# A three-norm macaron block in one software pipeline: the second FFN's gelu block and its products moved to other slots

## The chip, the cores and the metric

One core of a Trainium2 chip runs the whole program. The metric is the device time of one execution in microseconds (us), as the median over runs. TensorE (PE) multiplies matrices and writes to PSUM, VectorE (DVE), ScalarE (ACT) and GpSimd (POOL) do the elementwise work, SyncE (SP) issues the DMAs. Each engine works through its own queue strictly in order and meets the others at semaphores. All arithmetic on these queues is float32, except the bias and one-hot products.

## The reference, cut to what matters

The input is 32 sequences of 256 tokens with 128 features. It passes a mixture-of-experts FFN, a Mamba block (a selective scan) and the same FFN again:

```python
x = x + 0.5 * ffn(layernorm(x))     # f1
x = x + mamba(layernorm(x))         # p: the selective scan
x = x + 0.5 * ffn(layernorm(x))     # f2, same weights as f1
# ffn: e = argmax(x @ Wg + bg)      (8 experts)
#      y = gelu(x @ W1[e] + b1[e]) @ W2[e] + b2[e]
# mamba: x_path, z = split(rmsnorm(x) @ in_proj); x_path = silu(conv4(x_path))
#      dt_x, B, C = split(x_path @ x_proj); dt = softplus(dt_x @ dt_proj + b)
#      h = exp(dt*A)*h + dt*x_path*B ; y = C.h + D*x_path      (16 states, 256 channels)
#      out = (y * silu(z)) @ out_proj + x
```

## The kernel before

The 8192 tokens are cut into 16 chunks of 512. A hand-written software pipeline of 23 iterations (`i0` from -4 to 18) works on several chunks at a time: in iteration i the scan of chunk i, the Mamba preparation of chunks i+1 and i+2, the first FFN of chunks i+2 and i+3, and the second FFN of chunks i-1 to i-3. A stage that belongs to chunk i+off carries that `off`, and it is left out where the chunk does not exist. So iterations 3 to 12 carry all stages, and the later ones carry fewer and fewer.

Each iteration has 16 slots. In slot s, VectorE scans two units (2s and 2s+1) of the 32 that a chunk has; each unit is 128 partitions by 512 tokens. A unit is one `tensor_tensor_scan` (line 759, or line 757 in the slots of `POOL_C` = 1, 3, 5, 9, 14) and one product with C (line 763 on VectorE; in the slots of `POOL_C` line 944 on GpSimd). The decay of a unit, exp(dt*A), is made by ScalarE (line 632) in one of three PSUM buffers `dA`, so ScalarE can be at most three units ahead of VectorE. In its own slot s, ScalarE makes the decays of slot s+1. GpSimd makes the input of the units two slots ahead (line 936). TensorE sums the states (`sum_states`, line 489): at its slot s it sums what VectorE did in slots s-3 and s-2.

Everything else is placed between the units by tables. `PE_AT` (from `STAGES`), `ACT_AT`, `DVE_AT`, `POOL_AT` and `SP_AT` say at which slot each engine's queue holds a stage; a value of s+0.5 is behind the units of slot s. Each entry of `STAGES` is (name, offset, PSUM bank, slot, place in the slot); the two banks `G` are reused in the order of that list, and a stage waits until its bank was read. Place 0 is ahead of the slot's `sum_states`, place 1 too, place 2 at the end of the slot.

The FFN computes all eight experts for all tokens, and a one-hot mask that is added through the bias makes seven of them vanish. For each expert e of FFN w (0 for f1, 1 for f2) TensorE makes a first product (lines 461 and 462) into the only PSUM buffer `PH`, and ScalarE copies it out to `hs` (a "take", line 597) before the next first product may start. When all eight are taken, ScalarE runs a gelu block (`gelus`): table load, gelu of experts 0 to 3, one take between them, gelu of experts 4 to 7, table load back to exp. Then TensorE makes eight second products (line 477, 8 matmuls each, and line 475 for the bias at e = 0), which VectorE adds to X (line 815). `W1_AT` holds for each expert (slot and place of the first product on TensorE, slot and place of the take on ScalarE, offset), `W2_AT` (slot, place, offset) of the second product.

Other stages named below: `z0`, `z1` are the products for silu(z); `silu` is ScalarE's block of two table loads and three silus (lines 655 to 658); `out` is the output product of the Mamba block (line 511), which waits for bank 0 to be read by the first silu, and which VectorE adds to X at 4.5; `bc` and `dt1`, `dt0` are the products for B, C and dt (line 451); `soft` is the softplus; `ln_*` are the transposes of a normalized chunk and `gate_*` the expert logits (line 531), which VectorE turns into the one-hot mask `oh_*`; `x1`, `x0` are the products in front of the convolution, whose `taps` are made by ScalarE (line 647) and VectorE (line 776).

Of the kernel before, what the change touches and what calls it, by code (L numbers as in the profile page):

```python
# [46 lines left out]

STAGES = [("ln_f1", 3, 0, 1, 0), ("gate_f1", 3, 1, 2, 1), ("z0", 1, 0, 2, 2), ("z1", 1, 1, 3, 2),
# [3 lines left out]
PE_AT = {name: at for name, _, _, *at in STAGES}  # L52
G_SEQ = [(name, bank, off) for name, off, bank, _, _ in sorted(STAGES, key=lambda stage: stage[3:])]
G_AT = {name: (bank, off) for name, bank, off in G_SEQ}

ACT_AT = {"ln_f1": 1.5, "silu": 4.0, "bc": 6.0, "dt1": 6.5, "dt0": 7.0, "soft": 7.0, "gelu_f2": 7.5,
          "ln_f2": 9.5, "ln_p": 13.5, "taps": 14.5, "gelu_f1": 15.5}
DVE_AT = {"gated1": 1.5, "y_f2": 1.5, "gate_f1": 3.0, "out": 4.5, "oh_f1": 6.0, "stats_f2": 5.0, "gated0": 9.5,
          "y_f1": 10.0, "stats_p": 10.5, "gate_f2": 11.0, "stats_f1": 12.0, "oh_f2": 13.0, "tap01": 15.0, "tap2": 15.5}
POOL_AT = {"root_f2": 6.5, "norm_f2": 7.0, "dt": 8.0, "dtx": 8.5, "root_p": 11.0, "norm_p": 12.0, "root_f1": 12.5,  # L60
           "norm_f1": 13.0}
SP_AT = {"x_out": 3, "x_in": 4, "bc": 6, "b0": 8, "dt": 9, "b1": 10, "c0": 10, "b2": 12, "c1": 12, "b3": 14, "dtx1": 14,
         "c2": 14, "dt1": 15, "c3": 15}
# [967 lines left out]
```

## Time and profile before

| what | value |
|---|---|
| median of 3 runs | 1492.56 us (1492.42 to 1492.58) |
| the profiled execution | 1495.2 us, of which 1493.4 us is the span |
| TensorE / VectorE / GpSimd / ScalarE busy | 83% / 71% / 71% / 59% of the span |
| mean granted TensorE clock | 0.849 of full speed |
| one iteration, output product to output product | 82.4 to 82.8 us (iterations 2 to 12) |

The span runs from the first to the last instruction; the 1.8 us around it belong to the execution's time. The profiled execution is 2.6 us above the median of the three runs. A busy share is over the whole span, with the filling and the draining of the pipeline in it.

### The profile page before, as it was taken

Reading aid. Unit: us, or ns where it says so; the run is one execution under the profiler, and the core shown is the slowest. Engines: PE = TensorE matmul, PEld = TensorE weight load, DVE = VectorE, ACT = ScalarE, POOL = GpSimd, SP = SyncE. Lnnn points to the kernel's source line nnn. Section 1 sums busy time; section 2 is a strip of 40 time slices with the busy share of each in tenths; the row PEclk is TensorE's granted clock in tenths of the full one; section 3 lists DMA queues with packets and bytes.
Section 4 is the critical chain, followed back from the end, with each engine's and each line's share of the span. In section 5 each row is a group of like instructions: output and inputs, shape, how many; then the busy total and the mean of one; then the engine's idle time right before and its main releaser. Section 6 shows DMA issues by size and latency. Waiting matters only on the chain.

```text
span 1493.4 us, 16302 instructions
## 1 busy us (share of the span) xinstructions
PE 1232.2 (83%) x5188; PEld 612.7 (41%) x5188; DVE 1061.7 (71%) x1713; ACT 874.2 (59%) x1171; POOL 1067.6 (71%) x900
## 2 busy tenths in 40 slices
PE   2777768889898989989898988899898978667677
PEld 1333314234443534445353444444353434333344
DVE  2022887887878787877878787878878776979910
ACT  0244656476666767575667667575756675474532
POOL 1026796978878788868788787878687886997600
PEclk9989876788888998888888889888888987978786
DMA  3005050413233231503232332305032322232000
GB/s 84 1 0 205 10 198 9 158 43 120 92 108 106 89 111 33 181 23 127 80 120 92 108 106 73 127 24 185 28 115 85 122 85 105 101 114 92 1 7 14
DMA packets 60405, 130.02 MB, mean 87 GB/s; under 512 B 7744, under 2 KB 26864, under 8 KB 52128
## 3 DMA queue, kind: packets, MB, share of 16 engines
q1 hardware_dynamic: 60320, 128.98, 25.1%
q8 instruction: 42, 0.69, 0.2%
q14 instruction: 43, 0.35, 0.1%
HBM read 106.94 MB, written 22.02 MB: 86 GB/s over the span
## 4 chain that ended last, share of the span: by engine, by line
PE 41%; ACT 24%; DVE 23%; issue 8%; POOL 3%; SPq 1%; ACTq 0%; DVEq 0%; DMA 0%; POOLq 0%
PE PH L462 12%; PE PY L477 9%; DVE dA L759 9%; PE G L451 9%; ACT hs L610 6%; ACT dA L632 5%; DVE hb L757 4%; ACT hs L597 4%; DVE hb L763 3%; PE PH L461 3%; ACT L614 3%; ACT L610 2%; PE Y L489 2%; PE G L511 2%; PE G L531 2%
## 5 line engine op out<-in xcount | busy, mean ns | idle before, releaser
L936 POOL TENSOR_TENSOR hb<-dtx_rep,bs 128x1024 f32<-128x1024 f32 x256 | 598.8, 2361 | 0.0
L759 DVE TENSOR_TENSOR_SCAN dA<-dA,hb 128x512 f32<-128x512 f32 x352 | 429.8, 1221 | 68.5 <-ACT dA L632 61.6
L632 ACT ACTIVATE dA<-dt_rep,A 128x512 f32<-128x512 f32 x512 | 342.2, 689 | 143.4 <-DVE hb L763 128.7
L597 ACT COPY hs<-PH 128x512 f32<-128x512 f32 x256 | 149.4, 584 | 388.2 <-PE PH L462 387.9
L462 PE MATMUL PH<-xnT,W 128*128 128x512 f32 x512 | 339.0, 749 | 0.0
L477 PEld LDWEIGHTS PY<-W,hs 128*128 128x128 f32 x2048 | 281.8, 208 | 101.2 <-issue 88.8
L477 PE MATMUL PY<-W,hs 128*128 128x128 f32 x2048 | 323.2, 304 | 0.0
L944 POOL TENSOR_TENSOR hb<-hb,cs 128x1024 f32<-128x1024 f32 x80 | 188.4, 2355 | 140.7 <-DVE hb L757 140.7
L763 DVE TENSOR_TENSOR hb<-dA,cs 128x512 f32<-128x512 f32 x352 | 243.5, 692 | 25.2 <-DVE dA L759 0.9
L757 DVE TENSOR_TENSOR_SCAN hb<-dA,hb 128x512 f32<-128x512 f32 x160 | 186.3, 1206 | 102.6 <-ACT dA L632 99.5
L489 PE MATMUL Y<-hb,Sel 128*32 128x512 f32 x1024 | 164.5, 716 | 19.8 <-POOL hb L944 10.4
L461 PE MATMUL PH<-ohT,Lm 24*128 24x512 bf16 x256 | 109.1, 426 | 83.4 <-ACT hs L597 82.7
L610 ACT ACTIVATE hs<-hs 128x2048 f32<-128x2048 f32 x64 | 121.3, 1909 | 0.4
L462 PEld LDWEIGHTS PH<-xnT,W 128*128 128x128 f32 x512 | 86.6, 212 | 68.3 <-issue 68.3
L461 PEld LDWEIGHTS PH<-ohT,Lm 24*128 24x128 bf16 x256 | 23.5, 92 | 219.7 <-ACT hs L597 147.0
L776 DVE SCALAR_TENSOR_TENSOR xs<-G,Wc,xs 128x506 f32<-128x506 f32 (+2 forms) x96 | 67.2, 742 | 65.0 <-ACT xs L647 62.7
L531 PE MATMUL G<-Wg,xnT 128*128 128x8 f32 x256 | 56.2, 348 | 64.2 <-ACT xnT L590 64.2
L881 POOL TENSOR_SCALAR neg<-mv 128x4 f32<-128x4 f32 x48 | 9.7, 203 | 127.3 <-DVE mv L744 127.3
L963 POOL TENSOR_TENSOR dt<-dt,sp 128x1024 f32<-128x1024 f32 x16 | 37.6, 2353 | 83.5 <-ACT sp L676 83.5
L531 PEld LDWEIGHTS G<-Wg,xnT 128*128 128x128 f32 x256 | 53.8, 309 | 94.3 <-ACT xnT L590 94.0
L489 PEld LDWEIGHTS Y<-hb,Sel 128*32 128x32 f32 x1024 | 22.7, 116 | 114.1 <-issue 86.6
L815 DVE SCALAR_TENSOR_TENSOR X<-PY,X 128x512 f32<-128x512 f32 x32 | 21.8, 682 | 60.8 <-PE PY L477 60.8
(85 smaller groups left out, 1190.7 us busy)
## 6 DMA issues: line engine op xcount, KB each, us to landing
dtx_rep<-dtx_rows SPq DMA_DIRECT2D x32, 1024.0 KB, 6.5
dt_rep<-dt_rows SPq DMA_DIRECT2D x32, 1024.0 KB, 8.2
bs<-bc_rows SPq DMA_DIRECT2D x64, 256.0 KB, 3.7
cs<-bc_rows SPq DMA_DIRECT2D x64, 256.0 KB, 4.5
dtx_rows<-dtx SPq DMA_DIRECT2D x32, 256.0 KB, 2.5
dt_rows<-dt SPq DMA_DIRECT2D x32, 256.0 KB, 2.6
X<-in_x SPq DMA_DIRECT2D x16, 256.0 KB, 3.0
out<-X SPq DMA_DIRECT2D x16, 256.0 KB, 2.4
```

The costliest lines, as they stand in the source:

```text
L461: nc.tensor.matmul(PH[:, :], Lm[:, e, :], ohT[:, w, :], start=True, stop=False)
L462: nc.tensor.matmul(PH[:, :], W1[:, e, :], xnT[:, w, :], start=False, stop=True).then_inc(ph_full, 1)
L477: last = nc.tensor.matmul(PY[:, P * j:P * (j + 1)], hs[:, w, e, P * j:P * (j + 1)], W2[:, e, :], start=False, stop=e == E - 1 and j == J - 1)
L489: last = nc.tensor.matmul(Y[D32 * g:D32 * (g + 1), :], Sel[:, :], hb[:, (2 * k + g // 2) % HR, g % 2], start=q == 0, stop=q == NQ - 1)
L597: nc.scalar.copy(hs[:, w, e, :], PH[:, :]).then_inc(ph_free, 1)
L610: nc.scalar.activation(a, a, ACT.Gelu).then_inc(gelu[w], 1)
L632: nc.scalar.activation(dA[u % NA][:, :], dt_rep[:, h, g, :], ACT.Exp, scale=A[:, h, g, q:q + 1]).then_inc(decay, 1)
L757: nc.vector.tensor_tensor_scan(x_in_hb, a, x_in_hb, 0.0, ALU.mult, ALU.add).then_inc(scan, 1)
L759: nc.vector.tensor_tensor_scan(a, a, x_in_hb, 0.0, ALU.mult, ALU.add).then_inc(scan, 1)
L763: nc.vector.tensor_tensor(x_in_hb, a, cs[:, q, :], ALU.mult).then_inc(prod, 1)
L936: nc.gpsimd.tensor_tensor(hb[:, s % HR], dtx_rep[:, h, 2 * m:2 * m + 2, :], bs[:, q, None, :].broadcast_to([P, 2, CH]), ALU.mult).then_inc ...
L944: nc.gpsimd.tensor_tensor(hb[:, s % HR], hb[:, s % HR], cs[:, q, None, :].broadcast_to([P, 2, CH]), ALU.mult).then_inc(prod_p, 1)
```

## The change

Only tables change. No instruction is added or removed. On ScalarE the gelu block of f2 moves from slot 7.5 to slot 10.5, and `bc` and `dt0` move half a slot ahead. On TensorE the eight second products of f2 move from slots 10 to 15 to slots 12, 13, 14, 15 and to slots 0 and 1 of the next iteration (offset -3); `bc`, `dt1` and `dt0` stand directly behind `out`; `z1` stands ahead of the slot's `sum_states`; the first product of expert 6 of f2 stands ahead of `out`, and a first product of f1 stands at the end of slot 10, with its take inside the moved gelu block. On VectorE the addition of f2 moves from 1.5 to 2.5, and SyncE's store of x follows it.

```diff
-STAGES = [... ("z1", 1, 1, 3, 2),
-          ("out", -1, 0, 4, 1), ("oh_f1", 3, 1, 5, 1), ("bc", 1, 0, 6, 0), ("dt1", 1, 1, 6, 1),
-          ("dt0", 1, 0, 7, 0), ...
+STAGES = [... ("z1", 1, 1, 3, 1),
+          ("out", -1, 0, 4, 1), ("oh_f1", 3, 1, 5, 1), ("bc", 1, 0, 5, 0), ("dt1", 1, 1, 6, 0),
+          ("dt0", 1, 0, 6, 1), ...
-ACT_AT = {"ln_f1": 1.5, "silu": 4.0, "bc": 6.0, "dt1": 6.5, "dt0": 7.0, "soft": 7.0, "gelu_f2": 7.5,
+ACT_AT = {"ln_f1": 1.5, "silu": 4.0, "bc": 5.5, "dt1": 6.5, "dt0": 6.5, "soft": 7.0, "gelu_f2": 10.5,
-DVE_AT = {"gated1": 1.5, "y_f2": 1.5, ...
+DVE_AT = {"gated1": 1.5, "y_f2": 2.5, ...
-SP_AT = {"x_out": 3, ...
+SP_AT = {"x_out": 4, ...
-W1_AT = [[(8, 2, 7, 3, 3), (9, 2, 9, 0, 3), *[(s, 0, s, 0, 3) for s in (10, 11, 12, 13, 14, 15)]],
-         [(15, 1, 15, 0, -1), (15, 2, 15, 1, -1), (15, 3, 15, 3, -1), (1, 0, 0, 0, -2), (2, 0, 2, 0, -2),
-          (3, 0, 3, 0, -2), (5, 0, 4, 2, -2), (6, 0, 6, 0, -2)]]
-W2_AT = [[(s, 1, 2) for s in (4, 6, 8, 8, 8, 9, 9, 9)],
-         [(s, k, -2) for s, k in ((10, 1), (11, 1), (12, 1), (13, 1), (14, 1), (14, 1), (15, 1), (15, 2))]]
+W1_AT = [[(8, 2, 8, 0, 3), (9, 2, 9, 0, 3), (10, 0, 10, 0, 3), (10, 2, 10, 3, 3),
+          *[(s, 0, s, 0, 3) for s in (11, 12, 13, 14)]],
+         [(15, 0, 15, 0, -1), (15, 1, 15, 1, -1), (15, 2, 15, 3, -1), (1, 0, 0, 0, -2), (2, 0, 2, 0, -2),
+          (3, 0, 3, 0, -2), (4, 0, 4, 0, -2), (5, 0, 6, 0, -2)]]
+W2_AT = [[(s, 1, 2) for s in (5, 7, 7, 8, 8, 8, 9, 9)],
+         [(12, 1, -2), (13, 1, -2), (14, 1, -2), (15, 2, -2), (0, 1, -3), (0, 1, -3), (1, 1, -3), (1, 1, -3)]]
```

## Rows read from the trace of the kernel before

**Rows 1.** The page's first part: busy time, share of the span, instructions.

```profile
span 1493.4 us, 16302 instructions
...
PE 1232.2 (83%) x5188; PEld 612.7 (41%) x5188; DVE 1061.7 (71%) x1713; ACT 874.2 (59%) x1171; POOL 1067.6 (71%) x900
```

**Rows 2.** Windows: stretch, its us, busy us of PE, PEld, DVE, ACT, POOL, clock, DMA.

```profile
323.03:1148.25 825.22, 742.17 (x3241) 371.10 (x3241) 659.56 (x1060) 541.71 (x731) 667.09 (x561) 0.87 0.28 97
570.27:652.69 82.42, 73.69 (x324) 36.75 (x325) 65.99 (x107) 54.22 (x74) 66.74 (x57) 0.88 0.28 97
```

**Rows 3.** Waits in the iteration 570.27 to 652.69: total us, times, longest.

```profile
ACT hs L597 <- PE PH L462: 20.8, 11, 4.9
...
DVE hb L757 <- ACT dA L632: 7.4, 2, 4.2
...
DVE dA L759 <- ACT dA L632: 3.9, 3, 3.3
```

**Rows 4.** Timeline of VectorE, 565 to 655: start, us, instruction, idle before.

```profile
588.73 1.23 DVE L759 TENSOR_TENSOR_SCAN dA<-dA,hb 128x512 f32<-128x512 f32 x1 [3.29 <-ACT dA L632]
...
596.85 2.34 DVE L757 TENSOR_TENSOR_SCAN hb<-dA,hb 128x512 f32<-128x512 f32 x2 [4.23 <-ACT dA L632]
...
600.28 1.22 DVE L759 TENSOR_TENSOR_SCAN dA<-dA,hb 128x512 f32<-128x512 f32 x1
...
624.50 2.73 DVE L776 SCALAR_TENSOR_TENSOR xs<-G,Wc,xs 128x506 f32<-128x506 f32 x4 [2.29 <-ACT xs L647]
...
639.84 2.34 DVE L757 TENSOR_TENSOR_SCAN hb<-dA,hb 128x512 f32<-128x512 f32 x2 [3.15 <-ACT dA L632]
```

**Rows 5.** Timeline of ScalarE, 565 to 655.

```profile
584.67 0.69 ACT L668 ACTIVATE dt<-G,Bdt 128x512 f32<-128x512 f32 x1 [1.34 <-PE G L451]
...
589.32 1.28 ACT L610 ACT_TABLE_LOAD   x1
...
596.12 1.30 ACT L632 ACTIVATE dA<-dt_rep,A 128x512 f32<-128x512 f32 x2
...
618.76 0.58 ACT L590 COPY xrT<-G 128x512 f32<-128x512 f32 x1
...
631.83 1.28 ACT L610 ACT_TABLE_LOAD   x1
...
638.63 0.59 ACT L597 COPY hs<-PH 128x512 f32<-128x512 f32 x1
```

**Rows 6.** Timeline of TensorE, 565 to 655.

```profile
570.27 2.02 PE L511 MATMUL G<-Wo,y 128*128 128x128 f32 x16 [1.09 <-ACT zs L655]
...
591.04 1.06 PE L489 MATMUL Y<-hb,Sel 128*32 128x512 f32 x8
592.03 2.94 PE L477 MATMUL PY<-W,hs 128*128 128x128 f32 x24
594.91 0.38 PE L461 MATMUL PH<-ohT,Lm 24*128 24x512 bf16 x1
...
597.99 0.38 PE L461 MATMUL PH<-ohT,Lm 24*128 24x512 bf16 x1 [1.64 <-ACT hs L597]
...
639.27 0.38 PE L461 MATMUL PH<-ohT,Lm 24*128 24x512 bf16 x1 [2.27 <-ACT hs L597]
```

**Rows 7.** Windows as in rows 2, cut where the granted clock changes.

```profile
572.30:596.30 24.00, 24.00 (x126) 12.93 (x126) 15.88 (x26) 18.73 (x24) 19.24 (x16) 1.00 0.05 14
...
598.70:609.00 10.30, 10.30 (x33) 4.98 (x31) 9.64 (x25) 3.85 (x7) 6.68 (x10) 0.50 0.77 274
...
617.80:619.40 1.60, 0.06 (x2) 0.01 (x1) 1.57 (x3) 1.20 (x2) 1.42 (x4) 1.00 0.00 0
...
639.70:650.00 10.30, 9.53 (x23) 3.33 (x23) 9.63 (x16) 5.53 (x11) 6.98 (x3) 0.50 0.18 51
```

**Rows 8.** The output product two iterations from the full pipeline's end: TensorE, then VectorE.

```profile
1227.82 3.75 PE L511 MATMUL G<-Wo,y 128*128 128x128 f32 x16 [4.12 <-ACT zs L655]
...
1231.69 0.69 DVE L815 SCALAR_TENSOR_TENSOR X<-G,X 128x512 f32<-128x512 f32 x1 [1.75 <-PE G L511]
```

More of the change, by code:

```diff
@@ L45 @@
 FIRST, LAST = -4, NCH + 2
-STAGES = [("ln_f1", 3, 0, 1, 0), ("gate_f1", 3, 1, 2, 1), ("z0", 1, 0, 2, 2), ("z1", 1, 1, 3, 2),
[2 rows of a table removed]
+STAGES = [("ln_f1", 3, 0, 1, 0), ("gate_f1", 3, 1, 2, 1), ("z0", 1, 0, 2, 2), ("z1", 1, 1, 3, 1),
[2 rows of a table added]
           ("ln_p", 2, 0, 13, 0), ("x1", 2, 1, 14, 0), ("x0", 2, 0, 14, 1)]
@@ L54 @@
 G_AT = {name: (bank, off) for name, bank, off in G_SEQ}
-ACT_AT = {"ln_f1": 1.5, "silu": 4.0, "bc": 6.0, "dt1": 6.5, "dt0": 7.0, "soft": 7.0, "gelu_f2": 7.5,
+ACT_AT = {"ln_f1": 1.5, "silu": 4.0, "bc": 5.5, "dt1": 6.5, "dt0": 6.5, "soft": 7.0, "gelu_f2": 10.5,
           "ln_f2": 9.5, "ln_p": 13.5, "taps": 14.5, "gelu_f1": 15.5}
-DVE_AT = {"gated1": 1.5, "y_f2": 1.5, "gate_f1": 3.0, "out": 4.5, "oh_f1": 6.0, "stats_f2": 5.0, "gated0": 9.5,
+DVE_AT = {"gated1": 1.5, "y_f2": 2.5, "gate_f1": 3.0, "out": 4.5, "oh_f1": 6.0, "stats_f2": 5.0, "gated0": 9.5,
           "y_f1": 10.0, "stats_p": 10.5, "gate_f2": 11.0, "stats_f1": 12.0, "oh_f2": 13.0, "tap01": 15.0, "tap2": 15.5}
@@ L61 @@
            "norm_f1": 13.0}
-SP_AT = {"x_out": 3, "x_in": 4, "bc": 6, "b0": 8, "dt": 9, "b1": 10, "c0": 10, "b2": 12, "c1": 12, "b3": 14, "dtx1": 14,
+SP_AT = {"x_out": 4, "x_in": 4, "bc": 6, "b0": 8, "dt": 9, "b1": 10, "c0": 10, "b2": 12, "c1": 12, "b3": 14, "dtx1": 14,
          "c2": 14, "dt1": 15, "c3": 15}
-W1_AT = [[(8, 2, 7, 3, 3), (9, 2, 9, 0, 3), *[(s, 0, s, 0, 3) for s in (10, 11, 12, 13, 14, 15)]],
-         [(15, 1, 15, 0, -1), (15, 2, 15, 1, -1), (15, 3, 15, 3, -1), (1, 0, 0, 0, -2), (2, 0, 2, 0, -2),
-          (3, 0, 3, 0, -2), (5, 0, 4, 2, -2), (6, 0, 6, 0, -2)]]
-W2_AT = [[(s, 1, 2) for s in (4, 6, 8, 8, 8, 9, 9, 9)],
-         [(s, k, -2) for s, k in ((10, 1), (11, 1), (12, 1), (13, 1), (14, 1), (14, 1), (15, 1), (15, 2))]]
+W1_AT = [[(8, 2, 8, 0, 3), (9, 2, 9, 0, 3), (10, 0, 10, 0, 3), (10, 2, 10, 3, 3),
[4 more added lines that the diff above has]
+         [(12, 1, -2), (13, 1, -2), (14, 1, -2), (15, 2, -2), (0, 1, -3), (0, 1, -3), (1, 1, -3), (1, 1, -3)]]
 W1_ORDER = sorted((s, k, w, e, off) for w in range(2) for e, (s, k, _, _, off) in enumerate(W1_AT[w]))
```

2 rows, old and new, of the table STAGES are left out of this document.

## The prediction

> **What bounds the kernel now.** I read the busy shares first [rows 1]: TensorE is busiest at 83%, but that is the share of an engine that spends part of its time at half clock, so it bounds nothing by itself. The windows come next [rows 2]: ten full iterations take 825.2 us, 82.5 us each, and the one from 570.27 to 652.69 stands for them. In it VectorE is busy 66.0 us of 82.4. The waits [rows 3] and VectorE's timeline [rows 4] name what is missing: the reader is to see four large waits, all for ScalarE: 3.29 us at slot 8 (the softplus stands ahead of the decays), 4.23 us at slot 9 (the gelu block of f2), 2.29 us at the taps, 3.15 us at slot 1 (the gelu block of f1). These are 13.0 of the 16.4 us; the rest is small waits and the gaps between instructions. The scan queue on VectorE, held up by what ScalarE does between decays, sets the period. ScalarE waits 20.8 us for first products [rows 3], so TensorE is the next in line wherever its slack is thin.
>
> The clock belongs to this reading [rows 7]. Twice in the iteration it falls from 1.00 to 0.50 (2.4 to 1.2 GHz) for 10.3 us: behind an idle spell of 1.64 us at the gelu block of f2, and behind one of 2.27 us at that of f1 [rows 6]. It didn't fall behind the nearly idle 1.60 us at 617.8 [rows 7]. Spells of 3 us, of which the change makes new ones, I take to cost the clock as that of 2.27 does. At half clock the 16 matmuls of the output product take 3.75 us against 2.02 [rows 8, 6], a factor of 1.86. Today both stretches lie where TensorE has slack.
>
> **The change part by part.** All times are in the frame of this iteration. Full-clock durations of TensorE: a first product 1.45 us (594.91 to 596.36), an expert's second product 0.95 (2.94 for three, measured to the end), a sum 1.0 [rows 6].
>
> *The gelu block leaves slots 7.5 to 9.* It lasts from 589.32 to 596.12, 6.8 us [rows 5], and the 4.23 us go. What is late next is TensorE. From 572.3 to 596.3 it works without a gap [rows 7]; the new order holds the same work but for one first product, and begins with `bc`, which has to wait for bank 0 and so for VectorE's addition at 573.1. So the last first product ends at 573.1 + 24.0 - 1.4 = 595.8. Its take on ScalarE stands ahead of slot 10's decays: take 0.5, decay 0.7, and slot 10 starts at about 597.1 instead of 600.28 [rows 4]. In between dt0 comes 1.3 us earlier, because no second product stands between dt1 and dt0 (that is the 1.34 us wait in [rows 5]), and slot 9 waits about 0.9 us for a take. **Gain 3.1 us**, not 4.2; its bounds are 0 (if TensorE finds no faster order) and 4.2 + 1.3 = 5.5.
>
> *The block at slot 10.5.* It starts when slot 11's decays are made, about 600.0, and ends at 606.8. Until then VectorE has the rest of slot 10, the statistics of p, the gate, slot 11 and the statistics of f1, about 11.8 us from 597.1: to 608.8, past the block's end and two decays. So the block itself stalls VectorE by nothing. This cover is 1 to 1.5 us deep; without the gate and the statistics the block would cost about 4 us as it does now.
>
> The Trainium skill, page "ScalarE: Activation LUTs", section "What ACT_TABLE_LOAD costs", puts a switch of the function set at about 2.66 us, load and drain together. By that the block would be 2.8 us longer and some 1.5 us of it would show. The trace has 1.28 us for the load and the next instruction right behind it, so the sum goes by the trace.
>
> *What the block does to TensorE.* The first product of expert 3 is done at about 600.4; the next waits for the take between the gelus, at 603.5. That is 3.1 us idle, behind a gate of 8 narrow matmuls and another short spell: more than the 1.64 us behind which the clock falls today. So I expect 10.3 us at half clock from some time in 602 to 605. Then come, up to the first product at slot 13: first product, sum, one-hot transposes, first product, D product, second product with bias, ln_p transposes, first product, about 10 us at full clock, with 1 us of waiting in it. Done at 613.7 at full clock, at 617 at half clock for most of it. ScalarE's queue has that take ahead of the decays of slot 14 and of the copy of xrT. The copy came at 618.76 [rows 5]; it would come at 615.6 with the gain above, and comes at about 618.6. **Loss 2.9 us** (bounds 0 and 3.3): the 3.1 us are nearly used up when the taps start.
>
> *Slot 15 and slots 0, 1.* Now f2's first products have no second products between them. The one of expert 2 waits for the take of expert 1, which is behind decay 0, which waits for VectorE's unit 30. Before it TensorE is idle from 2.9 to 5.9 us behind the start of the taps: 3.0 us. Then it has to do, before ScalarE can make the decays of slot 1: first product, second product, sum, two second products (moved here), ln transposes, first product of expert 3, whose take stands ahead of the decays. That is 7.0 us at full clock, in the 8.2 us until the gelu block of f1 ends: 1.2 us to spare. With the clock fallen 1 to 3 us into it and at 1.86 times the length, it is done 17.0 to 17.8 us behind the start of the taps instead of 12.9, and the block ends at 14.1 (631.83 and 638.63 in [rows 5] are 7.3 and 14.1 behind 624.5). **Loss 3.3 us** when the clock falls, which I give nine times in ten: 3.0 us (bounds 0 and 3.8).
>
> *Slots 3 and 4.* `z1` now stands ahead of the sum and needs bank 1, which the gate on VectorE holds. Today TensorE is at half clock here and late (650.0 in [rows 7]); with the stretch moved forward it is early, and idle for 2.3 to 2.9 us before `z1`. If the clock falls again, it meets z1, sum, the first product of expert 6 (moved ahead of `out`) and `out`, 1 + 1 + 1.4 + 2.0 us at full clock, of which everything before `out` has to fit between the gate and the first silu, 3.9 us. At half clock `out` ends 2 to 3.6 us late, and VectorE's addition and `bc` with it. How such a case looks is shown [rows 8]: `out` at half clock took 3.75 us and VectorE waited 1.75 for it, without any first product ahead. **Loss 2.8 us** (bounds 0 and 3.8).
>
> *The rest at nothing.* The additions and the store of x move with slack: the store's DMA has more than half an iteration until its buffer is needed, and behind it in SyncE's queue stands a load for a chunk four iterations ahead. The second products at slots 12 to 15 lie beside VectorE's scans. GpSimd is busy 66.7 of 82.4 us and its order is the same.
>
> **The sum.** Per full iteration -3.1 + 2.9 + 3.0 + 2.8 = +5.6 us, on 11 iterations: +62. In the three draining iterations there are no first products of f1, so the waits for the block (at most 4.2 us each, 12.7 in all) go, against a later `out`; I put that at 7 us gained between bounds of 0 and 12.7, and the tail at 2 between -4 and 4, because its second products partly fill the waits for takes. So +53: the profiled execution goes from 1495.2 to 1548, and the median, 2.6 us lower, from 1492.6 to **1545**.
>
> **The rivals.**
> *The clock holds* (ends faster). Place: the 3.0 us spells at slots 10.5 and 15. If the clock stays at 1.00 through them, the three losses vanish, and the time is 1492.6 - 11 x 3.1 - 11 = 1447. For it speaks the spell of 1.60 us that cost nothing [rows 7]; against it the fall behind 1.64 [rows 6, 7]. It decides from the point where spells of 3 us leave the clock alone. Chance 0.16. The Trainium skill, page "TensorE: Matmul & The Clock Gate", section "HAM oscillation — how this bites in real kernels", ties the fall to longer waits than these, of 3 to 5 us for a DMA per tile; by it this rival wins, and the trace, where 1.64 us was enough, disagrees. Its next section tells of short idle spells between groups of matmuls that do the same, and with that the trace agrees.
> *Only the first stretch bites.* The 1.2 us to spare at slot 1 and the fit at slot 4 are enough: 11 x 0.2 and 9 us gained, 1481. Chance 0.14; for it speaks that the margins are my estimate, against it the factor of 1.86 on 7 us.
> *One of the two later ones bites.* 11 x (-0.2 + 2.9) - 9 = +21, 1513. Chance 0.15.
> *Nothing to see.* Gain and losses cancel within 3 us: inside the two cases above.
>
> **How the numbers follow.** The forecast case has 0.55, its own range is 1518 to 1578: the low end with half the slots 3 and 4 loss and the slot 1 loss seven times in ten, the high end with all three at their upper bounds (11 x 7.8 = 86). Faster by over 0.2% (which is about what a measurement can tell): the clock holds, and most of the second rival, 0.28; within 0.2%: 0.05; slower: 0.67. The range 1455 to 1572 leaves out the better half of the first rival and the top of the forecast case.
>
> **What would show it.** In the profile after: VectorE's wait at slot 9 falls from 4.2 to about 1 us, and a wait of ScalarE for line 462 stands there instead (right: the gain; wrong: still 3 us and more). A clock of 0.50 behind the moved block and again from the taps to slot 1: the mean clock falls below 0.849. The wait at slot 1 grows from 3.15 to over 6 us, and a take ahead of it waits for TensorE. VectorE waits 2 to 3 us for line 511 in slot 4. The prediction is wrong if the clock has only two stretches per iteration, or if the third falls where TensorE has time.

## The result, and the profile after

The changed kernel takes 1499.8 us (median of 20 runs, 1496.2 to 1519.7), the kernel before 1494.7 us beside it (20 runs, 1485.8 to 1499.4). The ratio is 1.0052, 95% interval 1.0032 to 1.0072: slower by half a per cent, where 3.5% was forecast. It lies inside the recorded range of 1455 to 1572. The profiled execution took 1498.55 us, with a span of 1496.8.

The page's first part of the changed kernel, as in [rows 1]:

```profile
span 1496.8 us, 16302 instructions
...
PE 1189.6 (79%) x5188; PEld 585.5 (39%) x5188; DVE 1063.1 (71%) x1713; ACT 868.6 (58%) x1171; POOL 1066.0 (71%) x900
```

The same work on every engine, but TensorE is busy 43 us less: it runs less time at half clock, not more. The windows of the ten full iterations, from one addition of the output product on VectorE to that of ten chunks later, and of one iteration:

```profile
336.08:1155.57 819.49, 703.39 (x3240) 348.04 (x3240) 660.81 (x1061) 537.04 (x731) 665.41 (x561) 0.92 0.29 97
664.09:746.01 81.92, 70.51 (x324) 34.81 (x324) 66.09 (x107) 53.72 (x74) 66.62 (x57) 0.92 0.29 98
```

81.9 us each, against 82.5 before, at a mean clock of 0.92 against 0.87 [rows 2]. So the full pipeline became a little *faster*. The loss is elsewhere. It shows in when VectorE adds the output product for the first time, which ends the filling phase:

```profile
241.93 0.69 DVE L815 SCALAR_TENSOR_TENSOR X<-G,X 128x512 f32<-128x512 f32 x1 [0.67 <-PE G L511]
```

```profile
255.02 0.69 DVE L816 SCALAR_TENSOR_TENSOR X<-G,X 128x512 f32<-128x512 f32 x1 [0.67 <-PE G L512]
```

The first row is of the kernel before, the second of the changed one: 13.1 us later. By the second addition it is still 10.9 us (325.2 and 336.1). With the other such rows the span divides so:

| part, by that addition | before | after | difference |
|---|---|---|---|
| filling, up to the 1st | 241.9 | 255.0 | +13.1 |
| 1st to 12th (11 steps) | 908.5 | 900.6 | -7.9 |
| 12th to 16th (draining) | 279.7 | 282.9 | +3.2 |
| tail, behind the 16th | 63.3 | 58.3 | -5.0 |
| span | 1493.4 | 1496.8 | +3.4 |

VectorE's timeline of one iteration after, which answers to [rows 4]:

```profile
671.69 0.41 DVE L813 COPY ohT<-G 24x512 bf16<-24x512 bf16 x1 [3.31 <-PE PY L478]
680.01 1.23 DVE L760 TENSOR_TENSOR_SCAN dA<-dA,hb 128x512 f32<-128x512 f32 x1 [0.32 <-ACT dA L633]
685.05 2.34 DVE L758 TENSOR_TENSOR_SCAN hb<-dA,hb 128x512 f32<-128x512 f32 x2 [1.15 <-ACT dA L633]
689.84 1.23 DVE L760 TENSOR_TENSOR_SCAN dA<-dA,hb 128x512 f32<-128x512 f32 x1 [1.27 <-ACT dA L633]
...
714.97 2.72 DVE L777 SCALAR_TENSOR_TENSOR xs<-G,Wc,xs 128x506 f32<-128x506 f32 x4 [2.87 <-ACT xs L648]
...
731.02 2.34 DVE L758 TENSOR_TENSOR_SCAN hb<-dA,hb 128x512 f32<-128x512 f32 x2 [3.87 <-ACT dA L633]
```

The two waits of 3.29 and 4.23 us became 0.32, 1.15 and 1.27, at slots 8, 9 and 10. But there is a new one of 3.31 us at slot 6, for TensorE, that the prediction does not have: the copy of f1's mask waits for the *second product of expert 0* of the chunk before, which still reads the old mask, and which the change moved from slot 4 to slot 5, behind `bc`. The prose of "The change" does not name this move, its diff does: the second products of f1 go from slots 4, 6, 8, 8, 8, 9, 9, 9 to 5, 7, 7, 8, 8, 8, 9, 9. The five large waits and the small one sum to 12.8 us, against 13.0 for four: the waits were exchanged, not removed.

Cut where the granted clock changes, as in [rows 7]:

```profile
693.40:693.90 0.50, 0.01 (x1) 0.00 (x0) 0.50 (x3) 0.50 (x1) 0.17 (x1) 1.00 0.77 279
693.90:700.70 6.80, 4.33 (x12) 1.03 (x13) 6.24 (x22) 6.76 (x8) 5.15 (x11) 0.50 0.62 235
700.70:716.40 15.70, 15.34 (x74) 7.08 (x69) 12.29 (x22) 8.32 (x14) 15.42 (x20) 1.00 0.23 68
...
721.00:725.00 4.00, 4.00 (x15) 2.61 (x19) 3.52 (x5) 3.45 (x3) 4.00 (x3) 0.57 0.42 160
...
735.00:738.40 3.40, 3.40 (x5) 0.60 (x3) 3.26 (x6) 0.69 (x1) 3.40 (x3) 0.52 0.00 0
```

There are three stretches at half clock, as forecast, but of 6.8, 3.4 and 3.4 us and not of 10.3 each (the last two windows take in a little of full clock, so their means are 0.57 and 0.52). TensorE's timeline shows the idle spells around them, at slots 10.5, 15 and 2:

```profile
696.37 0.60 PE L462 MATMUL PH<-ohT,Lm 24*128 24x512 bf16 x1 [2.95 <-ACT hs L598]
...
720.98 0.40 PE L462 MATMUL PH<-ohT,Lm 24*128 24x512 bf16 x1 [3.13 <-ACT hs L598]
...
733.54 1.06 PE L532 MATMUL G<-Wg,xnT 128*128 128x8 f32 x8 [0.67 <-ACT xnT L591]
```

The first stretch begins at 693.9, 0.5 us *into* the first spell (693.4 to 696.4), and ends 4.3 us behind it. So the spell of 2.95 us cannot be its cause as a whole, and some 2.5 of its 6.8 us lie where TensorE has nothing to do. The second begins at 721.2, right behind 3.13 us of idle time, the third at 734.9, in the middle of slot 2's work, behind 0.67 us of idle time and the gate.

### The profile page after: what moved, and what is told of

The parts are those of the page before. It is cut to its first block, busy times and chain, and to the rows that moved or that the text cites. A ratio compares the mean times of both kernels' runs of the same rounds, so it can differ in the third digit from the quotient of the medians.

```text
span 1496.8 us, 16302 instructions
## 1 busy us (share of the span) xinstructions
PE 1189.6 (79%) x5188; PEld 585.5 (39%) x5188; DVE 1063.1 (71%) x1713; ACT 868.6 (58%) x1171; POOL 1066.0 (71%) x900
## 4 chain that ended last, share of the span: by engine, by line
PE 51%; DVE 22%; ACT 17%; issue 6%; POOL 3%; SPq 1%; ACTq 0%; DVEq 0%; DMA 0%; POOLq 0%
PE PY L478 15%; PE PH L463 14%; PE G L452 8%; DVE dA L760 7%; PE Y L490 5%; ACT dA L633 5%; ACT hs L598 4%; DVE hb L758 4%; PE PH L462 4%; DVE hb L764 4%; ACT hs L611 3%; DVE xs L777 2%; PE Y L567 1%; PE G L444 1%; DVE X L816 1%
## 5 line engine op out<-in xcount | busy, mean ns | idle before, releaser
L478 PEld LDWEIGHTS PY<-W,hs 128*128 128x128 f32 x2048 | 272.8, 205 | 93.2 <-issue 83.9
L478 PE MATMUL PY<-W,hs 128*128 128x128 f32 x2048 | 307.6, 298 | 0.0
L490 PE MATMUL Y<-hb,Sel 128*32 128x512 f32 x1024 | 159.7, 696 | 32.9 <-POOL hb L945 21.8
L964 POOL TENSOR_TENSOR dt<-dt,sp 128x1024 f32<-128x1024 f32 x16 | 37.7, 2358 | 81.8 <-ACT sp L677 81.8
L532 PE MATMUL G<-Wg,xnT 128*128 128x8 f32 x256 | 41.2, 288 | 46.3 <-ACT xnT L591 46.3
L490 PEld LDWEIGHTS Y<-hb,Sel 128*32 128x32 f32 x1024 | 22.6, 115 | 112.6 <-issue 83.1
L532 PEld LDWEIGHTS G<-Wg,xnT 128*128 128x128 f32 x256 | 38.3, 230 | 70.5 <-ACT xnT L591 70.5
```

Source lines behind the costliest of these rows:

```text
L478: last = nc.tensor.matmul(PY[:, P * j:P * (j + 1)], hs[:, w, e, P * j:P * (j + 1)], W2[:, e, :], start=False, stop=e == E - 1 and j == J - 1)
L490: last = nc.tensor.matmul(Y[D32 * g:D32 * (g + 1), :], Sel[:, :], hb[:, (2 * k + g // 2) % HR, g % 2], start=q == 0, stop=q == NQ - 1)
```

## The experiments

Sixteen kernels ran, each with the kernel before on the same chip. "Step" is the mean of the ten steps between the 2nd and the 12th addition of the output product in the profiled execution; "1st" is the start of the first one, the end of the filling phase. For the kernel before these are 82.5 and 241.9, for the changed one 81.9 and 255.0. The "1st" is one value from one execution, and it moves by itself: e7 has the tables of the changed kernel and issues its zeros only after the 1st addition, yet it is at 252.2 against 255.0; e15 and e12 stand likewise at 251.1 and 255.1. Differences of up to some 4 us in that column are therefore not put down to a table here. The profiled execution can also lie off the median: e11's is 8 us below it and e8's 5, e3's is 5 us above it and e16's 4.

| run | median us | ratio to before (95%) | 1st | step |
|---|---|---|---|---|
| e1_bias_first | 1491.4 | 0.9981 (0.9965 to 0.9998) | 250.3 | 82.1 |
| e2_block_only | 1501.9 | 1.0051 (1.0023 to 1.0078) | 241.8 | 83.8 |
| e3_front_only | 1499.8 | 1.0034 (1.0003 to 1.0065) | 248.3 | 83.4 |
| e4_kept_busy | 1513.0 | 1.0127 (1.0109 to 1.0146) | 252.2 | 83.6 |
| e5_first_late | 1492.6 | 1.0002 (0.9984 to 1.0019) | 247.8 | 83.2 |
| e6_bias_late | 1498.2 | 1.0039 (1.0021 to 1.0057) | 252.3 | 82.7 |
| e7_kept_short | 1497.0 | 1.0033 (1.0014 to 1.0051) | 252.2 | 82.1 |
| e8_z1_back | 1480.6 | 0.9934 (0.9904 to 0.9964) | 248.8 | 80.9 |
| e9_z1_kept | 1461.1 | 0.9775 (0.9743 to 0.9807) | 249.6 | 78.9 |
| e10_mask_first | 1484.3 | 0.9933 (0.9909 to 0.9957) | 247.3 | 81.8 |
| e11_second_late | 1486.7 | 0.9960 (0.9938 to 0.9981) | 240.6 | 81.9 |
| e12_z1_alone | 1503.8 | 1.0069 (1.0044 to 1.0094) | 255.1 | 82.3 |
| e13_front_bare | 1503.4 | 1.0071 (1.0047 to 1.0095) | 243.9 | 83.1 |
| e14_kept_mask | 1457.0 | 0.9749 (0.9715 to 0.9783) | 250.1 | 78.9 |
| e15_kept_no_bias | 1493.9 | 0.9991 (0.9967 to 1.0016) | 251.1 | 81.9 |
| e16_kept_no_z1 | 1463.0 | 0.9791 (0.9757 to 0.9825) | 250.2 | 79.9 |

### The overlooked wait alone, and the two halves of the change

**e1_bias_first**, the changed kernel with one number back:

```diff
-W2_AT = [[(s, 1, 2) for s in (5, 7, 7, 8, 8, 8, 9, 9)],
+W2_AT = [[(s, 1, 2) for s in (4, 7, 7, 8, 8, 8, 9, 9)],
```

> The changed kernel with one entry put back: f1's second product of expert 0 at slot 4, directly behind the output product, instead of slot 5. Theory 1 (an overlooked wait): VectorE's copy of f1's one-hot mask at slot 6 waits for that product of the chunk before, 3.3 us in every full iteration, because the product now stands behind bc, a first product, the mask's transposes and a sum. Put back, the wait at slot 6 is gone, dt1 is no longer held by the copy (0.5 us) and TensorE fills the 0.95 us ahead of bc. As what follows is bound by TensorE's order up to slot 10, only 1.0 to 1.5 us per full iteration is won (82.0 to about 80.6 us), the rest comes back as a wait for ScalarE at slots 6 to 8; in all 10 to 16 us less than the changed kernel's 1499.8, so 1484 to 1490. Rival (the wait is the whole loss): 3.3 us per iteration, 36 us, 1464. Rival (the wait is covered by what follows): within 3 us of 1499.8.

**e2_block_only** is the kernel before with the block of f2 at slot 10.5, its second products, `y_f2`, `x_out` and the take of f1's expert 0 as in the change, and nothing of the front; **e3_front_only** is the changed kernel with these put back, and f1's first products too.

> The kernel before with the gelu block of f2 at 10.5, its second products at slots 12 to 1, its addition at 2.5 and nothing else; bc, dt, z1 and the first products stay where they were (only the take of f1's expert 0 leaves the block). Theory A (the front's order makes the trouble): no 3.3 us wait at slot 6, TensorE the bound up to slot 10, a full iteration of 80 to 81 us, 1475 to 1485 in all, and a filling phase like that of the kernel before. Theory B (the moved block makes the trouble, through the clock and the first products at slots 15 to 1): a full iteration no shorter than 82 us, 1495 or more, and the filling 8 to 13 us longer.

> The changed kernel with the gelu block of f2, its second products, its addition and the first products of f1 put back: what is left is bc and dt behind the output product, z1 ahead of the sum, f2's last two first products earlier and f1's first second product at slot 5. Theory A (the front's order makes the trouble): the 3.3 us wait at slot 6 is there and the block's 4.2 us wait at slot 9 too, in part (dt comes 1.3 us earlier): 82.5 to 84 us per iteration, 1500 to 1515, and most of the 13 us of the longer filling. Theory B: the front alone is neutral or gains 1 us per iteration: 1480 to 1494, and the filling is as long as before.

e1 gains 8 us on the changed kernel (1491.4 against 1499.8), less than Theory 1 said, and either half of the change alone loses about what the whole does. e3 shows 3.31 us at slot 6, as the changed kernel does, and e1 1.53 us there. But in e1 another wait came, of 1.8 to 2.2 us in five of the ten iterations; VectorE's timeline, then TensorE's:

```profile
739.41 0.69 DVE L816 SCALAR_TENSOR_TENSOR X<-G,X 128x512 f32<-128x512 f32 x1 [2.16 <-PE G L512]
```

```profile
731.03 2.07 PE L452 MATMUL G<-xrT,Wz 128*128 128x512 f32 x2 [1.91 <-DVEq L806]
733.04 1.94 PE L490 MATMUL Y<-hb,Sel 128*32 128x512 f32 x8
```

VectorE waits 2.16 us for the output product, because `z1`, now ahead of the sum, left TensorE idle for 1.91 us, and it, the sum and the first product behind it run at half clock (2.07, 1.94 and 2.08 us instead of 1.1, 1.0 and 1.1). That is the stall that the prediction put at slots 3 and 4. In the changed kernel it does not show: as I read it, VectorE comes late out of slot 6 there and TensorE has time. The steps of e1 lie between 80.4 and 84.6 us, mostly in turn.

The same place makes e2 slow. Its wait at slot 9 fell from 4.23 to 1.62 us, and four of its ten steps are 81.1 to 82.5 us; the other six are 84.6 to 86.1. In five of those TensorE, idle for some 3 us ahead of the output product, runs at half clock for 10.2 us behind that, and VectorE gets f1's mask late at slot 6. TensorE's timeline, then VectorE's:

```profile
655.69 2.83 PE L511 MATMUL G<-Wo,y 128*128 128x128 f32 x16 [2.98 <-ACT zs L655]
```

```profile
665.46 0.41 DVE L812 COPY ohT<-G 24x512 bf16<-24x512 bf16 x1 [2.53 <-PE G L540]
```

So neither theory on e2 held whole: its steps are no shorter than before, as Theory B said, and its filling phase is no longer, as Theory A said.

### Does the half clock cost anything?

**e4_kept_busy** and **e7_kept_short** are the changed kernel with matmuls of zeros in the spells at slots 10 and 15, six each in e4 and three in e7. They add zeros to the sum in `PY`, so the outputs are the same. The loop behind the second products of a place is (the value is 6 in e4):

```diff
+KEEP = {(10, 2): 3, (15, 1): 3}
...
+                        if (s, k) in KEEP and it.has(2) and it.has(-2):
+                            if s == 10:
+                                it.wait(pe, y_added[0], 2, 1, 1)
+                            for n in range(KEEP[s, k]):
+                                nc.tensor.matmul(PY[:, :], nil[:, :], xrT[:, :], start=s == 10 and n == 0,
+                                                 stop=s == 10 and n == KEEP[s, k] - 1)
```

> The changed kernel with 6 matmuls of a zero matrix added on TensorE behind the first product at the end of slot 10 and 6 more behind that at slot 15, in iterations 2 to 13, into the PSUM bank of the second products, to which they add nothing: 2.6 us each in the two idle spells of 3.0 and 3.1 us. If the clock's falls behind these spells cost what the prediction said (2.9 and 3.0 us per iteration), the iteration falls from 82.0 to about 77 us and the time by some 50 us. If they cost what the comparison of the traces says (0.9 and 0.7 us), the iteration falls to about 80.5 and the time to 1480 to 1487. If filling the spells delays the first products behind them, the time stays at 1495 to 1505 although the clock no longer falls there.

> The changed kernel with three matmuls of zeros (two passes of 0.43 us each, 2.6 us in all) in each of the two idle spells of about 3 us, at slots 10 and 15; the sums of the outputs are unchanged. e4_kept_busy had twice as many, which overran the spells. Theory A: the half clock that follows the two spells in the changed kernel costs nothing, since the wait at the taps is set by the copy of xr and its product and the one at slot 1 by ScalarE's queue; the steps stay at 81.7 to 82.2 us, the mean clock rises to about 0.92, and the time stays at 1495 to 1503 us. Rival B: the half clock costs what the taps and slot 1 lost, 0.9 + 0.7 us per iteration: steps of 80.3 us and 1480 to 1484 us.

e4 was badly sized: its six matmuls took 5.31 us, twice what I meant (each shows as two records of some 0.44 us), and overran the spells. VectorE's timeline of e7:

```profile
658.30 0.69 DVE L826 SCALAR_TENSOR_TENSOR X<-G,X 128x512 f32<-128x512 f32 x1 [2.16 <-PE G L515]
...
709.98 2.72 DVE L787 SCALAR_TENSOR_TENSOR xs<-G,Wc,xs 128x506 f32<-128x506 f32 x4 [2.30 <-ACT xs L657]
...
725.25 2.34 DVE L768 TENSOR_TENSOR_SCAN hb<-dA,hb 128x512 f32<-128x512 f32 x2 [3.09 <-ACT dA L642]
```

Both readings were half right. The waits at the taps and at slot 1 fell from 2.87 and 3.87 to 2.30 and 3.09 us: that is the half clock's price there, 1.35 us together. It was won at slot 1 in all ten iterations, at the taps in six; in the other four the clock fell at slot 10 all the same and the wait stayed at 2.88. And in the iteration shown the clock fell ahead of the output product instead: VectorE paid 2.16 us in slot 4, and waited 2.01 us at slot 8, against 0.32 in the others. The gain over the changed kernel is 3 us in 1500, and none of it is in the steps (82.1 against 81.9). My Theory A, that the clock costs nothing, came near in the time and was wrong in the reason; e9 settled that.

### z1, the mask and the clock: all eight combinations

**e8_z1_back** is e1 with z1 behind the sum again; **e12_z1_alone** the changed kernel with that alone; e9, e15 and e16 add the zeros of e7 to e8, e12 and e1.

```diff
-("z1", 1, 1, 3, 1)
+("z1", 1, 1, 3, 2)
```

> The kernel of e1_bias_first, with z1 back behind the sum in slot 3. In e1 TensorE idles 1.91 us before z1, and the half clock that is behind it makes the output product late: VectorE waits 1.8 to 2.2 us for it in most iterations. Theory A: the sum fills the idle spell, the output product comes up to 2 us earlier, the wait in slot 4 falls below 0.5 us, the steps go from 82 to about 80.5 us, and the time to 1474 to 1480 us. Rival B: VectorE's gain is given back at slot 6 or at slots 8 and 9, where ScalarE's takes wait for TensorE in any case; the steps stay at 81.5 to 82.5 us and the time at 1488 to 1494 us.

> The kernel of e8_z1_back with three matmuls of zeros (2.6 us) in each of the idle spells at slots 10 and 15, as in e7_kept_short. There the waits at the taps and at slot 1 fell to 2.30 and 3.09 us (2.87 and 3.87 in the changed kernel), but the output product came late in its place. Theory A: the half clock behind the two spells costs 0.6 us at the taps and 0.8 us at slot 1 per iteration; with the sum in front of z1 nothing is given back in slot 4, the steps go from 80.9 (e8) to about 79.6 us and the time to 1462 to 1470 us. Rival B: the half clock falls elsewhere again, in front of bc or the one-hot transposes, and the steps stay within 0.4 us of e8's: 1476 to 1484 us.

> The changed kernel with z1 back behind the sum in slot 3 and nothing else. The changed kernel has its 3.31 us wait for expert 0's second product at slot 6, and none for the output product. Theory A: z1's place costs nothing by itself while the mask wait stands, because ScalarE's takes at slots 8 and 9 are bound by TensorE's queue behind it: 1494 to 1500 us, steps of 81.5 to 82 us. Rival B: z1 ahead of the sum is a loss of its own, as between e1_bias_first and e8_z1_back (0.5 to 0.7%): 1486 to 1491 us.

> The changed kernel with z1 back behind the sum and the zeros in the two idle spells, expert 0's second product left in slot 5. Theory A: the price of the half clock (1.3 us per iteration at the taps and slot 1) shows as soon as the output product cannot be late, so z1's place alone hides it: steps of 80.3 to 80.7 us (81.9 less 1.3, the mask wait of 3.31 us stays), 1477 to 1483 us. Rival B: the mask wait hides it: steps of 81.9 us, 1495 to 1500 us.

> e1_bias_first with the zeros in the two idle spells, z1 left ahead of the sum. Theory A: the half clock then falls behind the idle spell in front of z1, and the output product comes 1.8 to 3 us late in part of the iterations: steps that change between 79 and 84 us, 1476 to 1488 us. Rival B: z1's place does not matter once the zeros are there: 1461 to 1465 us.

| us, median | expert 0 in slot 5 | expert 0 in slot 4 |
|---|---|---|
| z1 ahead, no zeros | 1499.8 (the change) | 1491.4 (e1) |
| z1 ahead, zeros | 1497.0 (e7) | 1463.0 (e16) |
| z1 behind, no zeros | 1503.8 (e12) | 1480.6 (e8) |
| z1 behind, zeros | 1493.9 (e15) | 1461.1 (e9) |

The left column moves by 10 us from end to end, the right one by 30. The 10 us, between e12 and e15, are clear of noise (1.0069 and 0.9991), but little of them is in the full pipeline. There the four kernels on the left have steps of 81.9, 82.1, 82.3 and 81.9 us, those on the right 82.1, 79.9, 80.9 and 78.9. So while VectorE waits for the mask, neither z1's place nor the clock is worth much in a full iteration. With expert 0 back in slot 4, filling the spells gives 28 us (e1 to e16) or 19 (e8 to e9), 20 to 22 of them in the ten steps either way. z1's place gives 11 us (e1 to e8); behind the zeros it gives 2 by the medians (e16 to e9), within their noise, and 11 by the steps of the profiled executions, where e16's was the slowest of its six. That stays open.

The expectation for e15 was wrong: z1's place does not uncover the clock's price, the mask does. e16's time, 1463.0, is what Rival B gave; its steps alternate as Theory A had it, but only between 79.2 and 81.0 us, with waits of 0.6 to 2.0 us for the output product.

Where the 3.25 us between e15 and e9 are, by VectorE's timeline of one iteration each, first e15:

```profile
669.98 0.41 DVE L823 COPY ohT<-G 24x512 bf16<-24x512 bf16 x1 [3.32 <-PE PY L481]
678.30 1.23 DVE L770 TENSOR_TENSOR_SCAN dA<-dA,hb 128x512 f32<-128x512 f32 x1 [0.32 <-ACT dA L642]
...
704.71 0.41 DVE L823 COPY ohT<-G 24x512 bf16<-24x512 bf16 x1 [0.57 <-PE PY L481]
714.03 2.72 DVE L787 SCALAR_TENSOR_TENSOR xs<-G,Wc,xs 128x506 f32<-128x506 f32 x4 [2.88 <-ACT xs L657]
```

and e9:

```profile
650.99 0.41 DVE L823 COPY ohT<-G 24x512 bf16<-24x512 bf16 x1 [1.53 <-PE G L544]
659.53 1.23 DVE L770 TENSOR_TENSOR_SCAN dA<-dA,hb 128x512 f32<-128x512 f32 x1 [0.53 <-ACT dA L642]
...
693.63 2.72 DVE L787 SCALAR_TENSOR_TENSOR xs<-G,Wc,xs 128x506 f32<-128x506 f32 x4 [2.33 <-ACT xs L657]
```

The mask wait gives 1.79 us and slot 8 takes 0.21 back. A further 0.55 at the taps, 0.57 at f2's mask and 0.3 at a scan ahead of it go with the clock, as I read it, and leave 0.25 us without a name: in e15 the clock still falls, in a place where the zeros don't reach. Its windows around slot 10:

```profile
669.98:689.50 19.52, 18.05 (x97) 10.43 (x98) 16.27 (x19) 10.82 (x17) 16.36 (x12) 1.00 0.23 76
689.50:697.00 7.50, 7.50 (x17) 3.66 (x16) 6.94 (x21) 7.46 (x8) 5.55 (x10) 0.54 0.87 326
697.00:714.03 17.03, 16.67 (x75) 7.57 (x73) 12.93 (x22) 9.10 (x16) 16.73 (x22) 1.00 0.18 48
```

The half clock fills 6.8 of the 7.5 us. It begins 0.6 us into the gate of 8 narrow matmuls, which has idle spells of 0.28 us right ahead of it and of 0.73 us ahead of the first product before, and TensorE is then busy without a gap. In e9 the same place has 3.4 us of it (a clock of 0.66 over 5.0 us of the windows). Why the fall is shorter there I can't say from these runs; only that it repeats: the steps of e15 are 81.92 to 81.94 us ten times in a row, those of e9 78.7 in nine of ten.

### What bounds slots 6 to 9

**e10_mask_first** and **e14_kept_mask** are e8 and e9 with f1's one-hot transposes ahead of `bc`:

```diff
-("oh_f1", 3, 1, 5, 1), ("bc", 1, 0, 5, 0)
+("oh_f1", 3, 1, 5, 0), ("bc", 1, 0, 5, 1)
```

> The kernel of e8_z1_back, with the one-hot transposes of f1 ahead of bc in slot 5, as in the kernel before (where bc is in slot 6). VectorE's copy of the mask at slot 6 waits 1.53 us for these transposes in e1, e5 and e8 and not at all in the kernel before. Theory A: this wait goes and is not given back (the waits at slots 8, 9 and 10 stay 0.5, 1.2 and 1.3 us): 1.5 us per full iteration, steps of 79.5 us, 1462 to 1468 us. Rival B: dt and the takes behind it come as late as now, the waits at slots 8 and 9 grow by what slot 6 gives, and the time stays at 1478 to 1484 us.

> e9_z1_kept with the one-hot transposes of f1 ahead of bc, as in e10_mask_first. In e10 the 1.53 us wait at slot 6 was gone, but 1.6 us of it came back at slot 8, and the rest of the iteration lost in irregular half-clock stretches. Theory A: slots 8 and 9 are bound by the takes of f1's first products, so slot 8's wait grows to about 2.1 us and the steps stay at 78.7 us: 1459 to 1463 us. Rival B: the gain of 1.5 us at slot 6 stays: 77.2 us, 1440 to 1446 us.

The 1.53 us at slot 6 are gone in both, and slot 8 waits 2.17 us instead of 0.5. VectorE's timeline of e14:

```profile
657.42 1.23 DVE L770 TENSOR_TENSOR_SCAN dA<-dA,hb 128x512 f32<-128x512 f32 x1 [2.18 <-ACT dA L642]
662.45 2.34 DVE L768 TENSOR_TENSOR_SCAN hb<-dA,hb 128x512 f32<-128x512 f32 x2 [1.14 <-ACT dA L642]
```

So slots 6 and 8 together cost 2.1 us in either order, set, as I read it, by what TensorE does for ScalarE between the output product and the takes. e14's steps are e9's, 78.9 us, as Theory A had it. e10 won nothing on e8 either: its steps alternate between 79.9 and 83.9 us, and the long ones have waits of 2.47 us at f2's mask and 5.17 us at slot 1. In the changed kernel slots 6 and 8 cost 3.31 + 0.32 = 3.63: the first 2.1 us of the mask wait are free, the last 1.5 are not. ScalarE's timeline in the changed kernel shows it waiting for first products in slots 8 and 9:

```profile
683.84 0.59 ACT L598 COPY hs<-PH 128x512 f32<-128x512 f32 x1 [3.25 <-PE PH L463]
...
688.63 0.59 ACT L598 COPY hs<-PH 128x512 f32<-128x512 f32 x1 [3.00 <-PE PH L463]
```

### The filling phase

**e6_bias_late** and **e11_second_late** are the kernel before with f1's second products of expert 0, or of experts 1 to 7, as in the change; **e13_front_bare** the kernel before with only z1, bc and dt moved; **e5_first_late** is e1 with f1's first products in their old slots.

```diff
 e6:
-W2_AT = [[(s, 1, 2) for s in (4, 6, 8, 8, 8, 9, 9, 9)],
+W2_AT = [[(s, 1, 2) for s in (5, 6, 8, 8, 8, 9, 9, 9)],
 e11:
+W2_AT = [[(s, 1, 2) for s in (4, 7, 7, 8, 8, 8, 9, 9)],
```

> The kernel of e1_bias_first, with the first products of f1's experts back in the slots of the kernel before (one per slot, 10 to 15, expert 7 behind the taps, and f2's first three one place later). Theory A: the filling phase is longer (250.3 us to the first addition of the output product in e1, 241.9 before) because the first products of f1 come earlier and block TensorE's queue in iterations where nothing else fills it; then the first addition comes at 242 to 245 us here, the steps stay at about 82 us, and the time is 1483 to 1487 us. Theory B: the filling phase is longer because of bc and dt directly behind the output product; then the first addition stays at 249 to 251 us and the time at 1490 to 1494 us.

> The kernel before, with one thing of the change alone: the second product of f1's expert 0 in slot 5 instead of slot 4. In the changed kernel VectorE's copy of f1's mask at slot 6 waited 3.31 us for that product. Theory A: the wait of about 3.3 us appears here too, is mostly taken up by the two waits behind it for ScalarE (3.29 us at slot 8, 4.23 us at slot 9, both of which shrink), and costs 0.3 to 0.9 us per iteration: 1498 to 1508 us. Rival B: it is added in full, 3.3 us on 14 iterations: about 1540 us. Rival C: it is taken up whole: 1494 to 1497 us. In the filling phase, Theory A expects the first addition of the output product up to 6 us later than 241.9 us.

> The kernel before, with one thing of the change alone: f1's second products of experts 1 to 7 in slots 7, 7, 8, 8, 8, 9, 9 (before: 6, 8, 8, 8, 9, 9, 9), that of expert 0 kept in slot 4. It asks what lengthens the filling phase: the first addition of the output product is at 241.9 us before, 241.8 with the gelu block moved alone, 252.3 with expert 0's second product late alone, 250.3 with everything but that, 247.8 with f1's first products put back as well. Theory A: these second products are not the cause, it is bc and dt and the banks of their sums: first addition at 241 to 243 us, steps 82.3 to 82.8, time 1491 to 1496 us. Rival B: they are: first addition at 245 to 249 us and time 1496 to 1502 us.

> The kernel before, with only bc, dt1, dt0 and z1 moved as the change moves them. Theory A: this lengthens the filling phase: first addition of the output product at 246 to 250 us instead of 241.9, steps of 82.4 us and less, 1494 to 1500 us. Rival B: the filling phase is as before, 241 to 243 us, and the loss there comes only with f2's experts 6 and 7 or expert 0 of f1: time 1485 to 1492 us.

e6 is the surest of them: one product one slot later ends the filling phase 10.4 us later, of which 5.6 are left at the second addition (330.8 against 325.2), and leaves the steps nearly alone (82.7 against 82.5), because with `bc` in slot 6 the mask waits only 0.48 us in the full pipeline. In the filling phase it waits long. VectorE's timeline of e6:

```profile
72.40 0.41 DVE L812 COPY ohT<-G 24x512 bf16<-24x512 bf16 x1 [4.59 <-PE PY L477]
...
99.72 4.27 DVE L776 SCALAR_TENSOR_TENSOR xs<-G,Wc,xs 128x506 f32<-128x506 f32 x6 [14.27 <-ACT xs L647]
```

The same two rows of the kernel before are at 70.76 and 96.05, those of the changed one at 72.33 and 102.74. So the copy of the mask is 1.6 us late at first, and the delay grows from row to row; which waits make it grow I did not take apart.

The clock has a part in it. Up to the first addition its mean is 0.86 before, 0.84 in the changed kernel and in e6. From the addition of `y_f1` to the taps shown it is 16.4 us before, 17.6 in e3, e5, e6 and e13, and 20.9 in e1 and the changed kernel, but 19.7 in e8, e10 and e12 and 17.3 in e15, although these have f1's first products in the same dense slots. They differ in the half clock that falls there: 10.2 us in the changed kernel, 6.8 in e8, e10 and e12, none in e15. Taken at the same 6.8 us, the dense slots cost 2.2 us (19.7 against 17.6). The rest of the attribution does not add up: bc, dt and z1 alone cost 2.0 us (e13), the gelu block and experts 1 to 7 nothing (e2, e11), expert 0's place 10.4 on the kernel before and 4.7 on the changed one (to e1), and f1's first products 2.5 (e1 to e5). Only the 10.4 is well outside what the 1st moves by itself. The parts overlap, and I did not take them apart further: that the change made the filling phase longer is shown, and that expert 0's place is a large part of it; how the 13.1 us divide is not.

e5 answered its own question halfway (the first addition at 247.8) and lost it all in the steps, 83.2 us, with waits of 1.0 and 3.1 us for the output product in turn. e11 was a surprise: f1's later experts as the change puts them are a gain of 0.4% on the kernel before, the wait at slot 8 falling from 3.29 to 2.39. e13 is a loss of 0.7% by itself: `bc` directly behind the output product makes the one-hot transposes and the mask 1.5 us late, and the wait at slot 9 stays at 4.23.

## Why the prediction was wrong

The direction was right, for a reason that is not the forecast's, so that was luck. The failed steps are the three losses by the clock, 8.7 us per iteration together, of which 1.6 came, and the filling phase, put at nothing, which cost 13.1 us. Measured between the same points of the iteration, the four terms are -2.1, +0.9, +0.7 and 0.0, in all -0.5 us, against -3.1, +2.9, +3.0 and +2.8 in the forecast. That the time lies within the recorded range proves nothing for the mechanism: none of the cases behind it (1447, 1481, 1513, 1545) took place. Step by step:

- **The block leaves slots 7.5 to 9, -3.1 us.** From the addition of the output product to slot 10 it is 25.75 us after against 27.87 before: 2.1 gained. The wait at slot 9 is 1.15 us, and ScalarE waits there for TensorE's first product, as it said. The mechanism was right; the sum was short of the mask wait, 1.5 us of which show (3.63 against 2.1). With expert 0 back in slot 4 the gain is 3.7 us (24.2 us to slot 10 in e9). And "slot 9 waits about 0.9 us for a take" was 1.15 and 1.27 us at slots 9 and 10.
- **The overlooked wait.** The prediction has no term for f1's second products: "the rest at nothing" names only those of f2, and asks only who takes their result. It did not ask what else waits for the *reader* of a buffer: the mask of the next chunk is copied over the one that this product reads. This is a step that was missing, not a size.
- **Slot 10.5, +2.9.** 0.9 came. The clock did fall, but for 6.8 us, of which some 2.5 lie in the spell itself; the copy of xr came 0.9 us late (19.4 us behind slot 10's start against 18.5) and not 3, and filling the spell gives 0.57 us at the taps.
- **Slots 15 to 1, +3.0.** The spell came (3.13 us), and the half clock behind it lasts 3.4 us and not 10.3. The wait at slot 1 is 3.87, not over 6; filling the spell brings it to 3.09. Mis-sized fourfold.
- **Slots 3 and 4, +2.8.** Nothing in the changed kernel, where TensorE idles 1.23 us before z1 and works at full clock from there to the output product. The third fall came earlier, at slot 2, where TensorE has time: that was one of the prediction's own signs of being wrong. In e1, e5, e7 and e16 the stall is real, of up to 2.2, 3.1, 2.2 and 2.0 us.
- **"The rest at nothing", filling phase included.** The sum has no term for the filling phase and gives no reason. It is 13.1 us, and the greatest term of the result.
- **Draining and tail, -9.** +3.2 and -5.0: the tail's 2 us came as 5, the draining phase's 7 us as a small loss. No run took these two apart.

The common error of the three clock terms is one step: every fall was given the 10.3 us of the two falls in [rows 7], and the whole 1.86 times on all that follows. With the terms measured at the taps and slot 1 the half clock costs 1.35 us in the iteration shown, not 5.9. Its price is hidden as well: 3 us in all by e7, 19 to 28 us (1.3 to 1.9%) once the mask wait is gone. So the first rival, *the clock holds*, did not happen. Filling its two spells was worth 2.0 to 2.2 us per full iteration at most, and not the 8.7 that the forecast took off; no run kept the clock up throughout (0.96 over the ten steps of e9). "Clock below 0.849" was wrong as a sign: it was 0.88. The Trainium skill, page "TensorE: Matmul & The Clock Gate", section "HAM oscillation — how this bites in real kernels", ties the fall to waits of 3 to 5 us for a DMA. The fall right behind 3.13 us agrees with that in length; the one 0.5 us into its spell, the one behind 0.67 us and a gate, and e15's behind 0.73 and 0.28 us and half a gate do not.

What the change holds of value comes out when two of its details are undone. e9 and e14, with the block at slot 10.5, expert 0 in slot 4, z1 behind the sum and the two spells filled, are 2.25% and 2.5% faster than the kernel before; e8, which is e9 without the zeros, is 0.66% faster. Only those 0.66% are the tables' alone: no run filled idle spells in the kernel before, so what zeros would give there is not shown.

## What to carry to other kernels

When a step is moved, list for it not only who waits for its result but who waits to overwrite what it reads; then walk the filling and draining phases by themselves, since a wait that is hidden in the full pipeline can show there. A gain or loss measured while a larger wait stands beside it says little on what it is worth: over ten full iterations, filling the same idle spells gave 4 us at most with the mask wait and 20 to 22 without it, so suspected costs should be tried in combination. And a fall of the clock is not a fixed price: look at how much of the half-clock stretch lies on work that somebody waits for. Last, know how far a single profiled number moves by itself before it is put down to an edit.

## What the runs showed of the hardware

- In the iterations shown, the half-clock stretches last 10.2 us in the kernel before and 6.8, 3.4 and 3.4 us in the changed one, behind idle spells of 1.64 and 2.27 us in the first and of up to 3.13 us in the second: the longer spell did not bring the longer stretch.
- A stretch can begin within an idle spell and spend part of itself there: in the changed kernel it begins 0.5 us into a spell of 2.95 us, and some 2.5 of its 6.8 us are idle.
- Narrow matmuls (the gate: eight of 128x8, 1.06 us in all at full clock) between short idle spells went with a fall in e15: it came 0.6 us into the gate, behind spells of 0.73 and 0.28 us, and the clock stayed at 0.50 for 6.8 us although TensorE was busy for all of them.
- The falls can repeat with the program's period: ten steps of e15 are 81.92 to 81.94 us, and e1's vary between 80.4 and 84.6 us with the same work in each.
- In the filling phase two kernels with the same tables there end it 2.8 and 4.0 us apart (the changed kernel and e7, e12 and e15), with half-clock stretches at other places.
- A float32 matmul of 128x512 with zeros shows as two records of about 0.44 us each (12 in 5.31 us).
